# Four transformer blocks on one core: the prologues of three attentions, their output buffers and the places of the mixture tiles

## What is computed

```python
x = x + L0_xattn(layernorm(x), ctx, ctx)     # 8 heads of 8 sequence rows, scale 8**-0.5
x = x + L0_ffn(layernorm(x))                 # ternary weights, quantized activations
x = x + L1_xattn(layernorm(x), ctx, ctx)     # as L0, with queries and keys of unit length, scale 5
x = x + L1_ffn(layernorm(x))                 # mixture of 8 experts, 2 chosen, and a shared one
x = x + L2_xattn(layernorm(x), ctx, ctx, gamma)   # as L0, times gamma
x = x + L2_ffn(layernorm(x))                 # mixture of 32 experts, 8 chosen, and a shared one
x = x + L3_xattn(layernorm(x), ctx, mask, ...)    # 16 heads, quantized weights
x = x + L3_ffn(layernorm(x))                 # mixture of 16 experts, 4 chosen, and a shared one
```

## Time and profile before

| | |
|---|---|
| median of 3 runs | 1391.78 us |
| the profiled execution | 1404.17 us, span of its core 1402.3 us |
| mean granted TensorE clock | 0.875 of full speed |
| PE (TensorE matmul) busy | 1123.6 us, 80% of the span |
| DVE, ACT, POOL busy | 649.0, 631.9, 581.4 us |
| DMA | 132.44 MB, mean 94 GB/s |

### The profile page before, as it was taken

How to read it: one execution, slowest core, us unless ns; L and a number is a source line. 1 busy time by engine, 2 the same in 40 slices (tenths; PEclk the granted TensorE clock), 3 DMA queues, 4 the chain that set the end, 5 groups by cost and what they waited for, 6 DMA issues and landing times. The chain is left out here.

```text
span 1402.3 us, 19238 instructions
## 1 busy us (share of the span) xinstructions
PE 1123.6 (80%) x6656; PEld 791.7 (56%) x6656; DVE 649.0 (46%) x1354; ACT 631.9 (45%) x996; POOL 581.4 (41%) x654
## 2 busy tenths in 40 slices
PE   2779723478849994798579999999877668999997
PEld 0445411333348882455268888888633456888886
DVE  5568478410163335677563333333476853333333
ACT  3456557446624432456443443334373433333432
POOL 3647500040116662423226656666401125666653
PEclk9989856778859996689869999999987869999999
DMA  5654130344413332444213335333110004333341
GB/s 156 185 159 143 60 106 0 77 125 128 110 42 117 108 91 56 105 120 122 69 41 106 113 113 175 105 105 112 44 17 1 1 24 138 115 105 105 108 119 54
DMA packets 66740, 132.44 MB, mean 94 GB/s; under 512 B 10907, under 2 KB 33883, under 8 KB 66038
## 3 DMA queue, kind: packets, MB, share of 16 engines
q1 hardware_dynamic: 65654, 131.23, 31.6%
q0 software_dynamic: 1024, 0.41, 0.1%
HBM read 115.55 MB, written 15.45 MB: 93 GB/s over the span
## 5 line engine op out<-in xcount | busy, mean ns | idle before, releaser
L1373 POOL TENSOR_TENSOR f_hid<-f_gated,f_coef 128x512 f32<-128x512 f32 x152 | 224.0, 1474 | 171.6 <-DVE f_gated L1404 159.7
L1404 DVE TENSOR_TENSOR f_gated<-f_act_g,f_p_u 128x512 f32<-128x512 f32 x152 | 104.4, 688 | 272.5 <-PE f_p_u L1236 266.7
L792 ACT ACTIVATE a_probs<-a_p_sc 128x1024 f32<-128x1024 f32 x192 | 188.7, 1017 | 58.6 <-PE a_p_sc L719 54.4
L890 DVE TENSOR_REDUCE a_maxes<-a_p_max 128x2 f32<-128x512 f32 x256 | 160.7, 682 | 81.1 <-PE a_p_max L686 80.9
L1313 ACT ACTIVATE f_hid_hi<-f_hid 128x512 fp32r<-128x512 f32 x152 | 96.0, 632 | 208.4 <-POOL f_hid L1373 208.3
L1408 DVE TENSOR_TENSOR f_hid_lo<-f_hid,f_hid_hi 128x512 fp32r<-128x512 f32 x152 | 106.1, 698 | 150.4 <-ACT f_hid_hi L1313 150.1
L1308 ACT ACTIVATE f_act_g<-f_p_g 128x512 f32<-128x512 f32 x152 | 90.7, 597 | 170.4 <-PE f_p_g L1236 170.4
L686 PE MATMUL a_p_max<-a_k,a_q 72*128 72x256 bf16 x512 | 99.1, 320 | 62.1 <-DMA a_q<-q_parts 44.3
L719 PE MATMUL a_p_sc<-a_q,a_k 75*128 75x256 bf16 (+1 forms) x768 | 129.1, 301 | 24.6 <-issue 10.3
L739 PE MATMUL a_p_out<-a_probs,all_v 128*32 128x256 f32 x1536 | 124.4, 444 | 13.0 <-ACT a_out L800 11.7
L1249 PE MATMUL f_p_y<-f_hid_hi,f_down_hi 128*128 128x512 f32 x304 | 120.1, 395 | 6.8 <-issue 6.8
(11 more groups left out here) (288 smaller groups left out, 1769.0 us busy)
## 6 DMA issues: line engine op xcount, KB each, us to landing
f_w<-in_w SPq DMA_DIRECT2D x76, 384.0 KB, 3.5
f_coef<-coef SPq DMA_DIRECT2D x51, 512.0 KB, 3.7
a_q<-q_parts SPq DMA_DIRECT2D x48, 288.0 KB
a_k<-k_plain SPq DMA_DIRECT2D x96, 96.0 KB
outs<-a_out SPq DMA_DIRECT2D x48, 128.0 KB, 3.7
a_whole<-outs SPq DMA_DIRECT2D x48, 128.0 KB, 2.6
a_k<-k_unit SPq DMA_DIRECT2D x24, 192.0 KB
all_v<-in_v SPq DMA_DIRECT2D x4, 1024.0 KB, 6.7
```

The lines of the kernel that those rows point to most:

```text
L792: nc.scalar.activation(probs[b % 2][:, 2 * pair:2 * pair + 2, :, :].rearrange("p h t d -> p h (t d)"), p_sc[pair % 2][:], ACT.Exp, scale=s ...
L890: nc.vector.tensor_reduce(maxes[b % 3][:, :, h], p_max[:, n % 3, :].rearrange("p (t d) -> p t d", t=NK), axis=AX.X, op=ALU.max, negate=Tru ...
L1373: nc.gpsimd.tensor_tensor(hid[c][:], gated[c][:], coef[slot(t, 2)][:, c * 512:(c + 1) * 512], ALU.mult).then_inc(hid_done, 1)
L1404: nc.vector.tensor_tensor(gated[c][:], act_g[c][:], p_u[c][:], ALU.mult).then_inc(gated_done, 1)
```

## The change

- `store_q` and `store_k` wait for all three parts of a group and store each tile (or half tile) with one DMA for its three parts.
- Layers 0 and 2: the casts of groups 2 to 4 move from POOL to ACT; POOL keeps the subtractions, in a new order, all before `split_max(1)`. `split_max(0)` comes after groups 2 and 3 (in layer 0 after all key groups too). On SP both halves of group 0 are stored before the first loads; groups 3 and 4 are stored in steps 0 and 1 instead of 1 and 3.
- Layer 0: the values are loaded over ACT's queue; `unit_keys.load` moves from step 0 to the end of step 2; ident and gamma are loaded before the first store.
- Layer 1: DVE squares every tile, and casts and splits groups 1 to 4 (`all_on_vector`), POOL none; three of the spreading matmuls stand before the first scores.
- Four output buffers instead of two. `load_whole(b - 3)` stands behind `store_out(b - 1)`; the reciprocals of DVE move back eight heads.
- gamma's tile is 128 bytes wide, and in the mixtures the small tiles are declared behind the large ones.

```diff
+    def all_on_vector(self, dve, g):
+        t, v = slice(*CUTS[g]), self.nc.vector
+        v.tensor_copy(self.part[:, 0, t, :], self.src[:, t, :]).then_inc(self.hi_ready[1], 1)
+        self.take_high(dve, v.tensor_tensor, g)
+        dve.wait_ge(*self.pick(self.rest_ready, g))
+        v.tensor_copy(self.part[:, 1, t, :], self.src[:, t, :]).then_inc(self.mid_ready[1], 1)
+        self.take_mid(dve, v.tensor_tensor, g)
...
     def total_others(self, pe):
-        pe.wait_ge(self.square_ready, 2)
         for i in range(1, NI):
+            pe.wait_ge(self.square_ready, i + 1)
...
+    OUTS = 4
...
                     for part in range(3):
                         parts.ready(sp, part, g)
-                        dst = bass.AP(m.q_parts.tensor, m.q_parts.offset + ((lo * 2 + b2) * 3 + part) * CH * ROW,
-                                      [[D, HEADS * CH], [6 * CH * ROW, hi - lo], [1, D]])
-                        sp.dma_start(dst, parts.part[64 * b2:64 * b2 + 64, part, lo:hi, :]
-                                     ).then_inc(q_stored[g][b2], 16)
+                    for i in range(lo, hi):
+                        dst = bass.AP(m.q_parts.tensor, m.q_parts.offset + (i * 2 + b2) * 3 * CH * ROW,
+                                      [[D, HEADS * CH], [CH * ROW, 3], [1, D]])
+                        sp.dma_start(dst, parts.part[64 * b2:64 * b2 + 64, :, i, :]).then_inc(q_stored[g][b2], 16)
...
                 for b in range(B):
-                    if b >= 2:
-                        load_whole(b - 2)
                     if layer == 1:
+                        if b in (0, 1, 2):
+                            store_q(b + 2, 0)
+                            store_q(b + 2, 1)
+                            load_q(2 * b + 4)
+                            load_q(2 * b + 5)
...
                     if b >= 1:
                         store_out(b - 1)
-                    if with_max and b in (1, 3):
+                    if with_max and b in (0, 1):
                         if layer == 0:
-                            store_k(b // 2 + 3)
...
+                            store_k(b + 3)
+                        store_q(b + 3, 0)
+                        store_q(b + 3, 1)
+                    if b >= 3:
+                        load_whole(b - 3)
+                    if layer == 0 and b == 2:
+                        unit_keys.load(sp, a)
...
-                    if b >= 2:
-                        act.wait_ge(out_stored[b % 2], 16 * (b // 2))
+                    if b >= OUTS:
+                        act.wait_ge(out_stored[b % OUTS], 16 * (b // OUTS))
...
+                    if layer == 0:
+                        key_parts.take_high(pool, tt, 0)
+                        key_parts.take_mid(pool, tt, 0)
+                        key_parts.take_high(pool, tt, 1)
+                        key_parts.take_high(pool, tt, 2)
+                        key_parts.take_mid(pool, tt, 1)
+                        key_parts.take_mid(pool, tt, 2)
+                        key_parts.take_high(pool, tt, 3)
+                        key_parts.take_high(pool, tt, 4)
+                        key_parts.take_mid(pool, tt, 3)
+                        key_parts.take_mid(pool, tt, 4)
+                    parts.take_high(pool, tt, 2)
+                    parts.take_high(pool, tt, 3)
+                    parts.take_mid(pool, tt, 2)
+                    parts.take_mid(pool, tt, 3)
                     split_max(0)
+                    parts.take_high(pool, tt, 4)
                     load_neg(0)
+                    parts.take_mid(pool, tt, 4)
                     split_max(1)
                     load_neg(1)
...
-        m.gamma = st.sb("gamma", [P, 1])
+        m.gamma = st.sb("gamma", [P, 32])
```

More of the change, by code:

```diff
@@ L142, in statistics, with tile_statistics, gather_statistics @@
     def statistics(self, dve, link, g):
+        lo, hi = self.groups[g]
+        for i in range(lo, hi):
+            last = self.tile_statistics(i)
+        self.gather_statistics(link, g, last)
+    def tile_statistics(self, i):
+        return self.nc.vector.bn_stats(self.stats[:, i, :], self.x[:, i, :])
+    def gather_statistics(self, link, g, last):
         v = self.nc.vector
         lo, hi = self.groups[g]
-        for i in range(lo, hi):
-            last = v.bn_stats(self.stats[:, i, :], self.x[:, i, :])
         link(last)
@@ L193 @@
 EPS2 = 1e-24
-def spread_one(one, cut):
-    return bass.AP(one[:].tensor, one[:].offset, [list(one[:].ap[0]), [0, cut[1] - cut[0]], [0, D]])
 class Parts:
@@ L447, in attention @@
         out_copied = st.sem("out_copied")
-        out_stored = [st.sem(f"out_stored{n}") for n in range(2)]
+        out_stored = [st.sem(f"out_stored{n}") for n in range(OUTS)]
         whole_loaded = [st.sem(f"whole_loaded{n}") for n in range(WHOLES)]
@@ L749, in _ @@
                     unit.total_others(pe)
+                    pe.wait_ge(masks_loaded[2], 16)
+                    for i in (1, 2, 3):
+                        unit.spread_out(pe, i)
                 n_max = n_turn = 0
@@ L769, in _ @@
                             scores(b, int(what))
-                            if layer == 1 and what == "1" and b < 4:
-                                if b == 0:
-                                    pe.wait_ge(masks_loaded[2], 16)
-                                for i in ((1,), (2, 3), (4, 5), (6, 7))[b]:
+                            if layer == 1 and what == "1" and 0 < b < 3:
+                                for i in ((4, 5), (6, 7))[b - 1]:
                                     unit.spread_out(pe, i)
@@ L820, in _ @@
                     parts.mid(act, 1)
-                    key_parts.mid(act, 2)
-                    for i in range(4, NI):
-                        norm.apply_by_act(i)
+                    act.wait_ge(norm.xn_by_act, 2)
+                    parts.high(2)
+                    key_parts.mid(act, 4)
+                    norm.apply_by_act(4)
+                    norm.apply_by_act(5)
+                    parts.mid(act, 2)
+                    act.wait_ge(norm.xn_by_act, 4)
+                    parts.high(3)
+                    norm.apply_by_act(6)
+                    norm.apply_by_act(7)
+                    parts.mid(act, 3)
+                    act.wait_ge(norm.xn_by_act, 6)
+                    parts.high(4)
                     copy_neg(0)
-                    key_parts.high(3)
-                    key_parts.mid(act, 3)
+                    parts.mid(act, 4)
                 elif layer == 2:
@@ L870, in _ @@
                             copy_neg(2)
+                        if layer == 0 and b in (1, 5, 9):
+                            load_v(b // 4 + 1)
                         if layer == 0 and b == 5:
@@ L919, in _ @@
                 if layer == 1:
-                    unit.square_first()
-                    norm.statistics(dve, link, 1)
+                    unit.square_of(0)
+                    for i in (1, 2, 3):
+                        norm.tile_statistics(i)
                     unit.clamp(dve, 0)
+                    for i in (4, 5):
+                        norm.tile_statistics(i)
+                    unit.invert(dve, 0)
+                    unit.scale_first(dve)
+                    norm.tile_statistics(6)
+                    parts.take_high(dve, tt, 0)
+                    norm.gather_statistics(link, 1, norm.tile_statistics(7))
+                    parts.take_mid(dve, tt, 0)
                     norm.refine(dve, link, 1)
@@ L1013, in _ @@
                 pool.wait_ge(ones_set, 2 if with_max else 1)
-                if layer == 0:
-                    for g in range(3):
-                        split_key(g)
                 if layer == 1:
-                    for g in range(1, len(CUTS)):
-                        pool.wait_ge(unit.out_ready, CUTS[g][1])
-                        parts.all_on_pool(pool, one, g)
                     for i in range(LATE):
```

209 lines of the change are left out of this document (97 added, 112 removed).

## The result

| | before | after |
|---|---|---|
| median of 20 runs | 1392.41 us (1387.33 to 1406.50) | 1385.19 us (1381.15 to 1389.34) |
| ratio, 95% interval | | 0.994 (0.992 to 0.996) |
| span of the profiled execution | 1402.3 us | 1380.5 us |
| mean granted TensorE clock | 0.875 | 0.880 |
| PE, DVE, ACT, POOL busy | 1123.6, 649.0, 631.9, 581.4 us | 1110.6, 664.3, 638.4, 551.0 us |

The change gains 7 us, not the 49 forecast, and 1385 lies outside the range of 1324 to 1368. The question is where some 40 us went. Comparisons between kernels of different rounds of runs are good to about 7 us: the kernel before, measured again beside each round, had medians from 1392 to 1400 us.

What follows compares the result with a forecast made beforehand. TensorE's matmuls were taken to bound the second mixture, waits the attentions. 27 - 2 + 5.5 + 8 + 10 = 48.5 us off 1404.17 gave 1355.7; that execution being 12.4 above the median, the forecast was 1343, range 1324 to 1368.

Steps and rivals of the forecast that it cites:

- part 4: Layer 2's prologue: earlier queries and fewer waits save 8 us (2 to 12); four buffers give nothing in layers 0 and 2.
- Part 1: Layer 1's steps: four output buffers and later whole-load remove store waits; 27 us (12 to 35), one step in four slow-clocked.
- Part 2: Layer 1's prologue: squares, casts and splits on DVE, spreading matmuls before first scores; 2 us lost (bounds -6 and +3).
- Part 3: Layer 0's prologue: earlier queries and negated maxima save 9 us, later unit keys lose 3.5; net 5.5 (-2 to +12).
- Part 5: Mixtures: aligned tiles make gate and up matmuls of layers 2 and 3 faster, 10 us (+11 to 9 lost).
- Rival (a): Layer 1's steps: transfers bind them, so half the gain or less comes, 1360 us; chance 0.14.
- (b): Mixtures: offsets are not the cause and the matmuls stay as they are, 1353 us; chance 0.15.
- (c): Mixtures: every matmul gets cheaper, down matmuls too, 20 us more, 1323 us; chance 0.05.
- Rival (d): Mixtures: the low clock takes them over after shorter attentions, making the kernel slower, 1426 us at ten tiles; chance 0.04.

Runs made afterwards that it cites:

- the mended kernel: The changed kernel with POOL's tile additions one step later and the unit keys loaded in step 0: 1323.97 us, ratio 0.945.
- the one with old steps: The changed kernel with layers 0 and 2's steps as before the change (two output buffers, earlier whole load, DVE's reciprocals from 53): 1340.95 us, ratio 0.959.
- this kernel: The mended kernel with two idle delays on POOL in layer 2, ahead of the maxima's split in steps 7 and 11: 1329.96 us, ratio 0.950.
- run 222: Not a follow-up run: "run" is a verb here, and 222 counts the matmuls that fit in 50 us.
- the thinner work: POOL, DVE and ACT work on layer 0's unit keys spread over more steps, against the mended kernel: 1309.55 us, ratio 0.938.

## Why the prediction was wrong

**The step that failed** is the last sentence of part 4: "In layers 0 and 2 the four output buffers give nothing: no copy waited for a store there, and the steps are TensorE's." In itself it is right (two buffers do as well), but it let the whole step loop pass at no cost, and with it the shift of DVE's reciprocals by eight maxima. The list of changes names that shift; the prediction put it at nothing, with no cost and no work that hides it. The question the prediction should have asked is the one it asked of SP: who waits for the moved instruction, and what is queued behind the one who waits. POOL's addition waits, and TensorE's maxima are queued behind it. The numbers to price it were there: four additions in each layer, a place at 73 against a need at 71. What the runs showed in its place: four waits of TensorE of 3.7 to 3.9 us in layer 0 and of 4.5 us in layer 2, with half clock behind them, 51 us by moving the addition (1385.19 to 1333.92) and 44 by undoing the shift with its whole load (to 1340.95).

**Part 1** was mis-sized: 35.9 us for 27. The steps take 4.38 us at a clock of 1.00 throughout, the upper bound of 35 that the prediction worked out and did not take, reading the low clock behind busy stretches in the earlier trace rows as a risk to one step in four. That reading was wrong. The two windows of the earlier trace rows leave out the microsecond between them, and in the kernel before TensorE stood still there (its timeline, 132 to 136 us):

```profile
134.15 1.03 PE L719 MATMUL a_p_sc<-a_q,a_k 75*128 75x256 bf16 x4 [1.64 <-DMA a_q<-a_neg_t]
```

The 0.50 came behind a wait, as in the experiments. The rule of the Trainium skill that was weighed there (TensorE: Matmul & The Clock Gate, "What's actually happening": activity releases the throttle) was the better guide in this stage: 63.00 of 65 us busy, at 1.00. Of the gain 12.5 us come with the rest of the change and not with the buffers. Rival (a) fell at a DMA share of 0.70.

**Part 2** said 2 us lost ahead of layer 1's first copy. That piece went from 115.0 to 114.5, and to 115.8 and 119.1 in the mended kernel and the one with old steps: between 0.5 us won and 4 lost, not told apart from nothing.

**Part 3** had the two terms wrong in opposite ways. Scores of layer 0 begin at 33.5 us, where 33 was forecast. The first copy comes 6.6 us earlier, and with the unit keys early the steps take 110.9 us for 114.4, a difference inside the spread of the old code (108.3 to 114.8): 7 to 10 us for the forecast 9. The unit keys cost 10 us (1333.92 - 1323.97), for 3.5 (whose own sum, 12 against 9, gives 3): the prediction let their landing overlap a step and a half of slack, but `split_max(5)`, which TensorE needs much sooner than batch 4's scores, stood behind them on POOL.

**Part 4**'s prologue gave 8.1 us ahead of the first copy (by the traces with 197 and 192 us there, 4 to 8). In the steps it gave 4.1 us with the old steps (102.3 to 98.2; the old code spreads from 99.8 to 106.4) and 8.1 with the new ones and the moved addition (99.1 to 91.0): about 8 to 16 us in all for 8.

**Part 5** held: 222 matmuls per 50 us and 9 to 12 us off (1394.35 - 1382.82 and 1394.35 - 1385.20), and the offsets were the cause as put. Rivals (b) and (c) fell: the gain was there, and twelve down matmuls of layer 3 take 2.72 us for 2.73.

**Rival (d)** named the low clock as what could turn the sign, but put it in the mixtures, where it was 1.00 in the two windows and 0.96 over 692 to 1000 us of the changed kernel, against 0.95 before. It struck in the attentions, and in the stretches read here behind waits.

The misses in the parts that were costed nearly cancel (9 us more in part 1, 6.5 less for the unit keys), so that the kernel with old steps comes out near 1343 is in part luck. The shift that was not costed took 44 to 51 us. The lower end of the range was also added up wrong: all parts at their better sides give 73 us and 1319, not 1322.

## What to carry to other kernels

List every instruction that a diff moves, on every engine, and write beside each who waits for it and what is queued behind that waiter: here a changed number on DVE, moved to suit a later load, delayed POOL's next duty and through it TensorE. When one engine's work moves later to fit a later producer, its consumers on in-order engines have to move too; here moving one call by one step gave 51 us. And where TensorE is nearly full, price each wait above its own length: here 1.7 to 2.1 times.

## What the runs showed of the hardware

- A wait of TensorE of only 1.12 us, in a stretch at full clock with 4.79 of 6 us busy, was followed by a stretch at 0.50; the step grew by 2.31 us. With 3.19 us it grew by 5.97. Shorter waits (0.36 to 0.77 us) in the last steps were followed by one in this kernel and by none in the mended one.
- The reverse: 65 us of steps with 63.00 us busy, and 88 us with 82.73, kept 1.00 throughout. The attention of layer 2 looked held by its clock (0.86) and was held by waits.
- Matmuls of 128x512 in fp32r whose weights and moving data start at the same offset modulo 128 bytes run 222 or 223 in 50 us, 0.225 us each, at offset 0 and at 32 alike. Where the gate and up matmuls have offsets 64 or 32 bytes apart it is 217 or 218, 0.230 us on the mean of gate, up and down.
- Two table loads of 1.28 us each around one root on ACT (0.42 us), with DVE's reciprocal queued on it, held TensorE for 4.4 us in the mended kernel's layer 0; with the reciprocal placed further behind the root, among the other moves of the thinner work, that wait was gone.
